# Closing a group of the GCN pass in steps between its turns, with the last layer's self edges taken from rows in SBUF

## The chip, the core and the metric

The kernel runs on one core of one Trainium2 chip. The metric is the device time of one execution in microseconds, lower is better. The engines are TensorE (PE), VectorE (DVE), ScalarE (ACT), GpSimd (POOL) and SyncE (SP); each works through its own instructions in order and waits for the others on semaphores.

## The reference, cut to what matters

A graph network over 12,500 nodes and 212,500 edges with 64 features: four layers, each of the form x = x + layer(relu(layernorm(x))). The change lies in the third layer and in what prepares the fourth:

```python
def _L2_gnn_ref(x, edge_index, W, b):          # third layer, GCN
    xw = x @ W
    norm = dis[src] * dis[dst]                 # src, dst with a loop for each node added
    out = segment_sum(norm[:, None] * xw[src], dst) + b
    return relu(out)

def _L3_gnn_ref(h, r, a, Wa_w, Wa_b, ...):     # fourth layer, four edge types
    cat = concatenate([h[dst], h[src]])
    gate = sigmoid(sum_i where(etype == i, cat @ r[i], 0))
    a_sc = sum(leaky_relu(cat @ Wa_w.T + Wa_b) * a[0])
    att = softmax of a_sc over the edges of a dst
    h_N = segment_sum(h[src] * att * gate, dst)
```

Among the fourth layer's edges are self edges (src equal to dst). The kernel does not gather those: it computes them for a whole block of nodes and opens the layer's running sums (`rel_state`, with the running maximum `rel_top`) with them.

## The kernel before

Nodes stand in 98 blocks of 128, one node a partition, sorted by degree. A block's edges are cut into chunks of four slots for 128 nodes; a chunk is fetched by four gathers (indirect DMAs that POOL issues, L973), each of one row per partition. Four chunks make a turn (RING = 4), and `got` holds the four chunks of a turn. SP loads a turn's lists of row numbers in two stages of two chunks (`load_lists`, L952) and its block numbers (`meta`, L957). DVE takes the chunks in order: it waits until one has landed, gives its list back (`list_used`), adds its four slots (L1709), gives the buffer back (`got_free`) and adds the sum to the block's state (L1712). SP's next list load waits for `list_used`, POOL for the list and for `got_free`.

The GCN pass (`gcn_edges`) does this first for the short chunks of two slots, then for the long ones. In the long part the turns are cut into 7 groups by blocks: when the turns of group g are done, the sums of 14 blocks are whole, and they are closed at once, as tiles of 128 x 896 (14 blocks of 64):

- `close(g)` on DVE: scale by `dis`, add the bias, relu and add to x (L1726 to L1729), then `relu_norm` (L405 to L414, with a square root on ACT in between), a copy to h (L1734), and the signal `h_ready`.
- PE transposes `hg` (L1793); for each of the 14 blocks it makes the source part `p_s` and the own part `p_w` of the last layer's rows (L1801 to L1803).
- ACT copies each block from PSUM into `rows` and `own` in SBUF (L1833 to L1839, the last raises `taken`) and sends them out as tables (L1841, L1843). There are seven such buffers.
- PE then makes the products of the self edges, `p_f`, with w_loop = w_src + w_own, two blocks in flight (L1808, L1810).
- `own_edges(g)` on DVE: for each block it takes p_f and makes the score and the gate (L1746 to L1755, with the four types' logits times `loop_type` and added up); then for all 14 the tanh on ACT (L1821) and the writes of `last_top` and `last_state` (L1759 to L1770).

DVE's order is written out: the turns of group g, then own_edges(g - 1), then close(g), then the turns of group g + 1. After the last group come own_edges(5), close(6) and own_edges(6), with no gathers beside them, and then the last layer (`rel_edges`), whose first gather needs the tables.

Of the kernel before, what the change touches and what calls it, by code (L numbers as in the profile page):

```python
# [7 lines left out]
ALU = mybir.AluOpType  # L8
# [113 lines left out]
def one_block(nc, eng):  # L122

    eng.addr_align(LOOP_SLOTS, max_nops=16)
# [15 lines left out]
def bc(ap, shape):  # L140
    return ap.to_broadcast(shape)
# [259 lines left out]
def relu_norm(nc, dve, ch, x, h, sq, st, shape, var_ready, std_ready, n):  # L401


    wide = lambda j: bc(st[:, j, :].unsqueeze(2), shape)
    ch.link(nc.vector.tensor_reduce(st[:, 0, :], x, AX, ALU.add))  # L405
    ch.link(nc.vector.tensor_scalar(st[:, 3, :], st[:, 0, :], 1.0 / D, None, ALU.mult))
    ch.link(nc.vector.tensor_tensor(h, x, wide(3), ALU.subtract))
# [3 lines left out]
    dve.wait_ge(std_ready, n)  # L411
    ch.link(nc.vector.reciprocal(st[:, 3, :], st[:, 2, :]))
    ch.link(nc.vector.tensor_scalar(sq, h, 0.0, None, ALU.max))
    ch.link(nc.vector.tensor_tensor(h, sq, wide(3), ALU.mult))  # L414
# [737 lines left out]
def load_weights(nc, k, a):  # L1152


    with ExitStack() as ctx:
# [55 lines left out]
        def _(dve):  # L1211
# [37 lines left out]
            ch.link(nc.vector.tensor_tensor(k.w_loop[:, :], k.w_src[:, :], k.w_own[:, :], ALU.add))  # L1249
# [103 lines left out]
def group_turns(eng, lists, g):  # L1353

    return (eng.value_load(lists.row_i[0:1, 9, bass.ds(g, 1)], min_val=0, max_val=CHUNKS // RING - 2),
            eng.value_load(lists.row_i[0:1, 9, bass.ds(g + 1, 1)], min_val=1, max_val=CHUNKS // RING - 2))
# [295 lines left out]
def gcn_edges(nc, k, part, state, table, after):  # L1652
# [4 lines left out]
    HELD = GROUP // 2  # L1657
    with ExitStack() as ctx:
# [3 lines left out]
        if after:  # L1662
            x, h, dis, bias, last_state, last_top = after
            logit, score = m.sb("logit", [P, TYPES, D]), m.sb("score", [P, D])
            gate, tanh = m.sb("gate", [P, GROUP, D]), m.sb("tanh", [P, GROUP, D])
            own_e, half_loop = m.sb("own_e", [P, GROUP]), m.sb("half_loop", [P, GROUP])
            p_f = [m.ps(f"p_f{j}", [P, OROW]) for j in range(2)]
            loop_made, loop_used = m.sem("loop_made"), m.sem("loop_used")
            gate_ready, tanh_ready = m.sem("gate_ready"), m.sem("tanh_ready")
            full = [P, GROUP, D]  # L1670
            Y, sq, hg = m.sb("Y", full), m.sb("sq", full), m.sb("hg", full)
            st = m.sb("st", [P, 4, GROUP])
# [4 lines left out]
            rows = [m.sb(f"rows{j}", [P, TYPES, RROW]) for j in range(HELD)]  # L1677
            own = [m.sb(f"own{j}", [P, OROW]) for j in range(HELD)]
# [3 lines left out]
            out = [m.sem(f"out{j}") for j in range(HELD)]  # L1682
# [14 lines left out]
        def _(dve):  # L1697
# [22 lines left out]
            def close(g):  # L1720
# [12 lines left out]
                relu_norm(nc, dve, ch, xb, hg[:, :, :], sq[:, :, :], st, full, var_ready, std_ready, g + 1)  # L1733
                ch.link(nc.vector.tensor_copy(h[:, blocks, :], hg[:, :, :]))  # L1734
                dve.sem_inc(h_ready, 1)

            def own_edges(g):
# [4 lines left out]
                for j in range(GROUP):  # L1742
                    z = j % 2
                    dve.wait_ge(loop_made, g * GROUP + j + 1)
                    dve.sem_inc(r.tick, 1)
                    ch.add(nc.vector.scalar_tensor_tensor(out=score[:, :], in0=p_f[z][:, 0:D], scalar=0.0,  # L1746
                                                          in1=k.att_a99[:, :], op0=ALU.max, op1=ALU.mult))
                    ch.link(nc.vector.tensor_tensor(logit[:, :, :], p_f[z][:, AW:].rearrange("p (t d) -> p t d", t=TYPES),
                                                    bc(k.loop_type[:, bass.ds(g * GROUP + j, 1), :]
                                                       .rearrange("p b t -> p (b t)").unsqueeze(2), [P, TYPES, D]),  # L1750
                                                    ALU.mult))
                    ch.add(nc.vector.tensor_reduce(own_e[:, j:j + 1], score[:, :], AX, ALU.add))
                    ch.link(nc.vector.tensor_reduce(gate[:, j, :], logit[:, :, :].rearrange("p t d -> p d t"), AX,
                                                    ALU.add))
                    ch.link(nc.vector.tensor_tensor(own_e[:, j:j + 1], own_e[:, j:j + 1], p_f[z][:, D:AW], ALU.add))  # L1755
                    dve.sem_inc(loop_used, 1)
                dve.sem_inc(gate_ready, 1)
# [15 lines left out]
            def group(g):  # L1773
                t0, t1 = group_turns(dve, lists, g)
                one_block(nc, dve)
                with dve.Fori(t0, t1) as i:
                    turn(i)

            group(0)
            close(0)  # L1780
            with dve.Fori(1, TURNS) as g:
                group(g)
                own_edges(g - 1)
                close(g)
            own_edges(TURNS - 1)

        if after:
            @block.tensor
            def _(pe):
                with pe.Fori(0, TURNS) as g:  # L1790
# [14 lines left out]
                    for j in range(GROUP):  # L1805
                        y, z = j % 2, j % 2
                        pe.wait_ge(loop_used, g * GROUP + j + 1)
                        nc.tensor.matmul(p_f[z][:, :], hT[y * D:(y + 1) * D, j // 2, :], k.w_loop[y * D:(y + 1) * D, :],  # L1808
                                         start=True, stop=False)
                        nc.tensor.matmul(p_f[z][:, 0:AW], k.ones[y * D:y * D + 1, :], k.own_bias[y * D:y * D + 1, 0:AW],  # L1810
                                         start=False, stop=True).then_inc(loop_made, 1)

            @block.scalar
            def _(act):
                act.sem_inc(taken, 2)
                act.sem_inc(loop_used, 2)
                for j in range(HELD):
                    act.sem_inc(out[j], 32)
                def tanhs(g):
# [3 lines left out]
                def group(g):  # L1823
# [4 lines left out]
                    for j in range(GROUP):  # L1828
                        z, w = j % 2, j % HELD
# [3 lines left out]
                        nc.scalar.activation(rows[w][:, :, 0:AW], bc(p_s[z][:, 0:AW].unsqueeze(1), [P, TYPES, AW]),  # L1833
                                             ACT.Copy)
                        nc.scalar.activation(rows[w][:, :, AW:AW + D],
                                             p_s[z][:, AW:].rearrange("p (t d) -> p t d", t=TYPES), ACT.Copy)
                        nc.scalar.activation(rows[w][:, :, AW + D:RROW], bc(hg[:, j:j + 1, :], [P, TYPES, D]), ACT.Copy,
                                             scale=0.5)
                        nc.scalar.activation(own[w][:, :], p_w[z][:, :], ACT.Copy).then_inc(taken, 1)  # L1839
                        act.wait_ge(taken, g * GROUP + j + 3)  # L1840
                        act.dma_start(by_rank(k.rel_tab)[:, blk, :], rows[w][:, :, :].rearrange("p t c -> p (t c)")  # L1841
                                      .unsqueeze(1)).then_inc(out[w], 16)
                        act.dma_start(k.own_tab[blk].rearrange("a p c -> p (a c)"), own[w][:, :]).then_inc(out[w], 16)  # L1843
# [6 lines left out]
                for j in range(HELD):  # L1850
                    act.wait_ge(out[j], 64 * TURNS + 32)
# [457 lines left out]
def gnn_program(nc, a, out):  # L2309
    ctx = ExitStack()  # L2310
    with ctx:
# [34 lines left out]
        k.w_loop = m.sb("w_loop", [P, OROW])  # L2346
# [139 lines left out]
```

## Time and profile before

| | |
|---|---|
| median of 3 runs | 13329.96 us (13327.62 to 13337.75) |
| profiled execution | 13332.53 us, its span 13330.8 us |
| busy in the span | POOL 64%, DVE 47%, PE 17%, ACT 13%, PE weight loads 11% |
| GCN pass, gathers | 1640, from 8576.0 to 10813.4 us |
| last layer, first gather | 10947.8 us |

Busy shares are means over all layers, which have different limits; what a stop costs is read from the timeline of its own stretch. In the rows below an instruction stands with its start, its duration, its engine, its line, what it writes and reads, and in brackets how long the engine was idle before it and what ended that.

### The profile page before, as it was taken

To read this page: it belongs to the slowest core of one execution; us is meant where nothing else is said; L and a number is where in the kernel's file an instruction comes from. 1 tells how busy PE (TensorE), PEld (TensorE's weight loads), DVE (VectorE), ACT (ScalarE), POOL (GpSimd) and SP (SyncE) were. 2 spreads that over 40 slices of the span, in tenths; PEclk is the share of its full clock that TensorE was granted. 3 is DMA by queue.
4 is the path that set the end of the run, shared out by engine and by line. 5 is a ranking of instruction groups with operands and counts; after the bars stand their busy time and mean duration, and the time that the engine had idled before them with its cause. 6 is when DMAs were issued, how large, how long until landed. Compare 5 with 4: busy or idle time off the path is not lost. (4 is left out here: it accounts for less than half of the span.)

```text
span 13330.8 us, 107772 instructions
## 1 busy us (share of the span) xinstructions
PE 2243.3 (17%) x7664; PEld 1456.1 (11%) x7664; DVE 6297.5 (47%) x21149; ACT 1706.1 (13%) x5627; POOL 8506.9 (64%) x8805
## 2 busy tenths in 40 slices
PE   8730000000000000000000000012222233333334
PEld 6620000000000000000000000001111112222223
DVE  9992333333344444444444444312222237777765
ACT  0000000000001000000011111000000014444443
POOL 0017466677656767776767777676666647777775
PEclk9755555555555555555555555555555555555555
DMA  0001233333311222222111111122222224444442
GB/s 10 0 14 39 28 27 27 26 29 28 27 21 29 32 33 33 33 33 31 26 25 27 27 27 27 26 49 47 47 47 48 48 52 107 108 107 107 107 101 64
DMA packets 1006418, 574.69 MB, mean 43 GB/s; under 512 B 757826, under 2 KB 855635, under 8 KB 1005953
## 3 DMA queue, kind: packets, MB, share of 16 engines
q0 software_dynamic: 307520, 409.04, 18.8%
q1 hardware_dynamic: 587723, 101.69, 4.7%
q10 hardware_dynamic: 111088, 63.12, 1.6%
q14 instruction: 71, 0.58, 0.0%
q8 instruction: 16, 0.26, 0.0%
HBM read 485.71 MB, written 87.37 MB: 43 GB/s over the span
## 5 line engine op out<-in xcount | busy, mean ns | idle before, releaser
L973 POOL DMA_INDIRECT got<-gat_tab,list x3280 | 3113.8, 949 | 1323.4 <-issue 970.7
L973 POOL DMA_INDIRECT got<-rel_tab,list x1640 | 1648.0, 1005 | 709.3 <-issue 448.4
L973 POOL DMA_INDIRECT got<-gcn_tab,list x1640 | 1548.5, 944 | 740.6 <-issue 495.7
L973 POOL DMA_INDIRECT got<-h_tab,list x1640 | 1567.9, 956 | 676.1 <-issue 492.4
L1709 DVE TENSOR_REDUCE chunk_sum<-got 128x64 f32<-128x256 f32 (+1 forms) x436 | 239.7, 550 | 1577.2 <-DMA got<-gcn_tab,list 1492.7
L1059 DVE TENSOR_TENSOR prod<-got,h 128x256 f32<-128x256 f32 (+1 forms) x436 | 179.6, 412 | 1309.2 <-DMA got<-h_tab,list 1203.5
L1641 PE MATMUL p_t<-ident,hg 128*128 128x128 f32 x98 | 24.6, 429 | 4436.6 <-DVEq L1546 4436.6
L1446 DVE COPY e<-top 128x4 f32 (+1 forms) x872 | 189.3, 217 | 1224.1 <-DMA got<-gat_tab,list 966.6
L535 POOL DMA_INDIRECT info_tab<-info,rank_i x98 | 125.4, 1279 | 977.1 <-DVEq L512 947.5
L2204 PE MATMUL p_gate<-got,ident 128*128 128x256 f32 (+1 forms) x872 | 510.3, 689 | 1382.8 <-DVE gate L2041 1382.8
L1588 ACT ACTIVATE p<-e 128x20 f32<-128x20 f32 (+3 forms) x872 | 185.4, 213 | 3719.1 <-DVE e L1465 3536.9
L358 PE MATMUL counts<-hot 125*128 125x98 bf16 x3400 | 608.3, 356 | 70.6 <-DVE hot L256 70.6
L2041 DVE COPY_PREDICATED gate<-is_t,own 128x256 f32<-128x256 int32 (+1 forms) x1308 | 553.9, 423 | 45.2 <-issue 35.4
L1430 DVE SCALAR_TENSOR_TENSOR type_of<-list 128x4 f32<-128x4 int32 (+1 forms) x436 | 72.9, 167 | 965.8 <-DMA got<-gat_tab,list 908.1
L1641 PEld LDWEIGHTS p_t<-ident,hg 128*128 128x128 f32 x98 | 19.0, 223 | 4439.3 <-DVEq L1546 4439.3
L358 PEld LDWEIGHTS counts<-hot 125*128 125x128 bf16 x3400 | 478.1, 142 | 199.7 <-DVE hot L256 86.2
L1486 DVE TENSOR_REDUCE chunk_sum<-prod 128x68 f32<-128x272 f32 (+3 forms) x872 | 494.4, 567 | 1.1
L2174 ACT ACTIVATE value<-got,msg 128x64 f32<-128x64 f32 x1640 | 439.2, 336 | 14.1
L2206 PE MATMUL p_gate<-gate,ident 128*128 128x256 f32 (+1 forms) x872 | 440.3, 609 | 0.0
L1299 PE MATMUL p_t<-ident,staged 128*128 128x128 f32 x49 | 23.2, 473 | 2446.2 <-ACT staged L1315 2442.5
L2035 DVE TENSOR_TENSOR feat<-got,own 128x256 f32<-128x256 f32 (+1 forms) x436 | 179.0, 411 | 536.3 <-DMA got<-rel_tab,list 516.6
L2204 PEld LDWEIGHTS p_gate<-got,ident 128*128 128x128 f32 x872 | 218.2, 310 | 1674.6 <-DVE gate L2041 1674.6
(436 smaller groups left out, 8709.3 us busy)
## 6 DMA issues: line engine op xcount, KB each, us to landing
own<-own_tab SPq DMA_DIRECT2D x436, 160.5 KB, 2.4
got<-gat_tab,list POOLq DMA_INDIRECT x3280
rel_tab<-rows ACTq DMA_DIRECT2D x98, 386.0 KB, 2.9
got<-h_tab,list POOLq DMA_INDIRECT x1640
got<-gcn_tab,list POOLq DMA_INDIRECT x1640
got<-rel_tab,list POOLq DMA_INDIRECT x1640
own_tab<-own ACTq DMA_DIRECT2D x98, 160.5 KB, 3.4
chunks_src<-rows_src SPq DMA_DIRECT2D x480, 4.5 KB
```

What stands on the lines that cost most here:

```text
L358: last = nc.tensor.matmul(counts[j][:, :], hot[:, h, 0:P, t], hot[:, h, P:P + BLOCKS, t], start=False, stop=False, skip_group_check=True)
L973: pool.indirect_dma_start(r.got[:, q, j, :], None, table, at(r.lists[s][:, c, j:j + 1]))\
L1059: return ts.add(nc.vector.tensor_tensor(prod[:, :, :], r.got[:, q, :, 0:D], bc(own_hn[:, bass.ds(b[q], 1), :], [P, S, D]), ALU.mult))
L1446: ts.add(nc.vector.tensor_copy(e[:, z, S, :], top[:, blk, :].rearrange("p b h -> p (b h)")))
L1486: return ts.add(nc.vector.tensor_reduce(chunk_sum[:, :], prod[:, :, :].rearrange("p s f -> p f s"), AX, ALU.add))
L1588: nc.scalar.activation(p[:, q % 2, :, :], e[:, q % 2, :, :], ACT.Exp).then_inc(p_ready, 1)
L1709: ts.link(nc.vector.tensor_reduce(chunk_sum[:, :], r.got[:, q, :, :].rearrange("p s f -> p f s"), AX, ALU.add))
L2035: nc.vector.tensor_tensor(feat[:, q, :, :], r.got[:, q, :, 0:D], bc(own[:, q, 0:D].unsqueeze(1), [P, S, D]), ALU.add)\
L2041: ins = nc.vector.copy_predicated(gate[:, q, :, :], bc(is_t[:, t, q, :].unsqueeze(2), [P, S, D]), bc(own[:, q, AW + (t + 1) * D:AW + (t + ...
L2174: last = nc.scalar.activation(value[:, q, j, :], r.got[:, q, j, AW + D:RROW], ACT.Copy, scale=msg[:, q, j, D:AW])
L2204: nc.tensor.matmul(p_gate[z][:, :, :], k.ident[:, :], r.got[:, q, :, AW:AW + D], start=True, stop=False)
L2206: nc.tensor.matmul(p_gate[z][:, :, :], k.ident[:, :], gate[:, q, :, :], start=False, stop=True)\
```

## The change

`relu_norm` is split in two, `norm_variance` (up to the variance) and `norm_scale` (from the reciprocal on). A group's closing is no longer done at once, but in five steps between the turns of the next group: `sums` ahead of its first turn, `scale` after the first, `own_half` for seven blocks after the fourth, `own_half` for the other seven after the fifth, and `own_edges` after the sixth. Six turns of a group are therefore written out in the loop over groups, and the rest stays an inner loop. `h_ready` comes before the copy to h. `own_half` takes the score and gate of the self edges from `rows` and `own` in SBUF, which ACT fills anyway, for seven blocks (128 x 448) at a time, and picks the type with predicated copies. The products p_f, w_loop and their semaphores are gone; `rows` and `own` hold all 14 blocks.

```diff
-def relu_norm(nc, dve, ch, x, h, sq, st, shape, var_ready, std_ready, n):
+def norm_variance(nc, ch, x, h, sq, st, shape, var_ready):
...
+def norm_scale(nc, ch, h, sq, st, shape):
...
-            ch.link(nc.vector.tensor_tensor(k.w_loop[:, :], k.w_src[:, :], k.w_own[:, :], ALU.add))
...
-            rows = [m.sb(f"rows{j}", [P, TYPES, RROW]) for j in range(HELD)]
-            own = [m.sb(f"own{j}", [P, OROW]) for j in range(HELD)]
+            rows, own = m.sb("rows", [P, GROUP, TYPES, RROW]), m.sb("own", [P, GROUP, OROW])
...
-            def close(g):
+            def sums(g):
...
                 dve.wait_ge(taken, g * GROUP + 2)
                 dve.sem_inc(r.tick, 1)
-                relu_norm(nc, dve, ch, xb, hg[:, :, :], sq[:, :, :], st, full, var_ready, std_ready, g + 1)
-                ch.link(nc.vector.tensor_copy(h[:, blocks, :], hg[:, :, :]))
+                norm_variance(nc, ch, xb, hg[:, :, :], sq[:, :, :], st, full, var_ready)
+
+            def scale(g):
+                dve.sem_clear(close_step)
+                ch = Chain(dve, close_step)
+                dve.wait_ge(std_ready, g + 1)
+                dve.sem_inc(r.tick, 1)
+                norm_scale(nc, ch, hg[:, :, :], sq[:, :, :], st, full)
                 dve.sem_inc(h_ready, 1)
+                ch.link(nc.vector.tensor_copy(h[:, bass.ds(g * GROUP, GROUP), :], hg[:, :, :]))
+
+            def own_half(g, half):
+                js = slice(half * HALF, (half + 1) * HALF)
+                dve.sem_clear(close_step)
+                ch = Chain(dve, close_step)
+                dve.wait_ge(taken, g * GROUP + ((half + 1) * HALF + 2))
+                dve.sem_inc(r.tick, 1)
+                tt = nc.vector.tensor_tensor
+                ch.add(tt(score[:, :, :], rows[:, js, 0, 0:D], own[:, js, 0:D], ALU.add))
+                ch.add(nc.vector.tensor_copy(of_type[:, :, :],
+                                             k.loop_type[:, bass.ds(g * GROUP + half * HALF, HALF), :]))
+                ch.link(tt(gate[:, js, :], rows[:, js, 0, AW:AW + D], own[:, js, AW:AW + D], ALU.add))
+                ch.add(nc.vector.scalar_tensor_tensor(out=score[:, :, :], in0=score[:, :, :], scalar=0.0,
+                                                      in1=bc(k.att_a99[:, :].unsqueeze(1), [P, HALF, D]),
+                                                      op0=ALU.max, op1=ALU.mult))
+                for t in range(1, TYPES):
+                    ch.link(tt(logit[:, :, :], rows[:, js, t, AW:AW + D],
+                               own[:, js, AW + t * D:AW + (t + 1) * D], ALU.add))
+                    ch.link(nc.vector.copy_predicated(gate[:, js, :],
+                                                      bc(of_type[:, :, t].unsqueeze(2), [P, HALF, D]).bitcast(I32),
+                                                      logit[:, :, :]))
+                ch.link(nc.vector.tensor_reduce(own_e[:, js], score[:, :, :], AX, ALU.add))
+                ch.link(tt(own_e[:, js], own_e[:, js], rows[:, js, 0, D], ALU.add))
+                ch.link(tt(own_e[:, js], own_e[:, js], own[:, js, D], ALU.add))
...
-                for j in range(GROUP):
-                    z = j % 2
-                    dve.wait_ge(loop_made, g * GROUP + j + 1)
...
-            group(0)
-            close(0)
-            with dve.Fori(1, TURNS) as g:
-                group(g)
-                own_edges(g - 1)
-                close(g)
+            t0, t1 = group_turns(dve, lists, 0)
+            one_block(nc, dve)
+            with dve.Fori(t0, t1) as i:
+                turn(i)
+            with dve.Fori(1, TURNS) as g:
+                t0, t1 = group_turns(dve, lists, g)
+                sums(g - 1)
+                turn(t0)
+                scale(g - 1)
+                turn(t0 + 1)
+                turn(t0 + 2)
+                turn(t0 + 3)
+                own_half(g - 1, 0)
+                turn(t0 + 4)
+                own_half(g - 1, 1)
+                dve.sem_inc(gate_ready, 1)
+                turn(t0 + 5)
+                own_edges(g - 1)
+                one_block(nc, dve)
+                with dve.Fori(t0 + 6, t1) as i:
+                    turn(i)
+            sums(TURNS - 1)
+            scale(TURNS - 1)
+            own_half(TURNS - 1, 0)
+            own_half(TURNS - 1, 1)
+            dve.sem_inc(gate_ready, 1)
             own_edges(TURNS - 1)
...
-                    for j in range(GROUP):
-                        y, z = j % 2, j % 2
-                        pe.wait_ge(loop_used, g * GROUP + j + 1)
-                        nc.tensor.matmul(p_f[z][:, :], hT[y * D:(y + 1) * D, j // 2, :], k.w_loop[y * D:(y + 1) * D, :],
-                                         start=True, stop=False)
...
-                        act.wait_ge(out[w], g * 64 + (32 * (j // HELD) + 32))
+                        act.wait_ge(out[j], g * 32 + 32)
```

## Rows read from the trace of the kernel before

**Rows 1.** The page: busy time of the engines (us, share, instructions); the costliest groups
```profile
PE 2243.3 (17%) x7664; PEld 1456.1 (11%) x7664; DVE 6297.5 (47%) x21149; ACT 1706.1 (13%) x5627; POOL 8506.9 (64%) x8805
...
L973 POOL DMA_INDIRECT got<-gcn_tab,list x1640 | 1548.5, 944 | 740.6 <-issue 495.7
```

**Rows 2.** Waits of POOL, 8830 to 10947: total us, times, longest us
```profile
POOL got L973 <- DMA list<-chunks_rank: 177.9, 18, 34.5
```

**Rows 3.** Timeline, closing after group 1: start us, us, instruction [idle before, releaser]
```profile
9103.51 0.22 DVE L1712 TENSOR_TENSOR gcn_state<-gcn_state,chunk_sum 128x64 f32 x1 [0.24 <-DVE chunk_sum L1709]
...
9120.11 0.94 POOL L973 DMA_INDIRECT got<-gcn_tab,list  x1 [0.30 <-issue]
...
9151.61 0.58 DVE L1709 TENSOR_REDUCE chunk_sum<-got 128x64 f32<-128x256 f32 x1 [4.48 <-issue]
...
9153.01 2.83 SPq L952 DMA_DIRECT2D list<-chunks_rank  x2
...
9155.57 0.94 POOL L973 DMA_INDIRECT got<-gcn_tab,list  x1 [34.52 <-DMA list<-chunks_rank]
...
9158.58 0.94 POOL L973 DMA_INDIRECT got<-gcn_tab,list  x1 [2.07 <-issue]
```

**Rows 4.** Timeline, closing after group 0
```profile
8901.27 0.23 DVE L1712 TENSOR_TENSOR gcn_state<-gcn_state,chunk_sum 128x64 f32 x1 [0.24 <-DVE chunk_sum L1709]
...
8904.19 1.82 POOL L973 DMA_INDIRECT got<-gcn_tab,list  x1 [0.30 <-issue]
...
8907.57 1.04 POOL L973 DMA_INDIRECT got<-gcn_tab,list  x1 [0.30 <-issue]
...
8910.07 0.17 DVE L410 TENSOR_SCALAR st<-st 128x14 f32<-128x14 f32 x1
...
8912.72 0.63 DVE L1734 COPY h<-hg 128x896 f32<-128x896 f32 x1
...
8917.72 0.58 DVE L1709 TENSOR_REDUCE chunk_sum<-got 128x64 f32<-128x256 f32 x1 [4.38 <-issue]
...
8921.60 0.94 POOL L973 DMA_INDIRECT got<-gcn_tab,list  x1 [1.75 <-DMA list<-chunks_rank]
```

**Rows 5.** Timeline, gathers beside a closing of the second GAT layer
```profile
6881.04 1.76 POOL L973 DMA_INDIRECT got<-gat_tab,list  x1 [0.30 <-issue]
...
6889.34 1.17 POOL L973 DMA_INDIRECT got<-gat_tab,list  x1 [0.30 <-issue]
```

**Rows 6.** Groups by line and form, GCN pass and last layer: busy us, mean ns
```profile
L1748 DVE TENSOR_TENSOR logit<-p_f,loop_type 128x256 f32<-128x256 f32 x98 | 40.6, 415 | 0.0
...
L1753 DVE TENSOR_REDUCE gate<-logit 128x64 f32<-128x256 f32 x98 | 56.4, 576 | 0.0
...
L409 DVE TENSOR_REDUCE st<-sq 128x14 f32<-128x896 f32 x7 | 7.6, 1086 | 0.2
...
L2041 DVE COPY_PREDICATED gate<-is_t,own 128x256 f32<-128x256 int32 x1152 | 507.3, 440 | 38.7 <-issue 35.4
```

**Rows 7.** Timeline, end of the pass, DVE, PE, ACT and POOL
```profile
10815.82 0.23 DVE L1712 TENSOR_TENSOR gcn_state<-gcn_state,chunk_sum 128x64 f32 x1 [0.24 <-DVE chunk_sum L1709]
...
10847.76 1.09 DVE L1726 TENSOR_TENSOR Y<-gcn_state,dis 128x896 f32 x1 [0.29 <-DVE rel_state L1770]
...
10859.48 1.76 PE L1793 MATMUL p_t<-ident,hg 128*128 128x128 f32 x7 [17.50 <-DVEq L1735]
...
10905.94 0.44 ACT L1839 ACTIVATE own<-p_w 128x321 f32<-128x321 f32 x1
...
10934.25 0.15 DVE L1755 TENSOR_TENSOR own_e<-own_e,p_f 128x1 f32<-128x1 f32 x1
...
10937.02 1.09 DVE L1770 TENSOR_TENSOR rel_state<-gate,half_loop 128x896 f32<-128x896 f32 x1
...
10947.81 0.94 POOL L973 DMA_INDIRECT got<-rel_tab,list  x1 [134.40 <-DMA list<-chunks_rank]
```

**Rows 8.** DMA queues, 8830 to 10947: packets, MB, share of 16 engines
```profile
q14 instruction: 10, 0.08, 0.0%
```

More of the change, by code:

```diff
@@ L1663, in gcn_edges @@
             x, h, dis, bias, last_state, last_top = after
-            logit, score = m.sb("logit", [P, TYPES, D]), m.sb("score", [P, D])
-            gate, tanh = m.sb("gate", [P, GROUP, D]), m.sb("tanh", [P, GROUP, D])
+            logit, score = m.sb("logit", [P, HALF, D]), m.sb("score", [P, HALF, D])
+            of_type = m.sb("of_type", [P, HALF, TYPES])
             own_e, half_loop = m.sb("own_e", [P, GROUP]), m.sb("half_loop", [P, GROUP])
-            p_f = [m.ps(f"p_f{j}", [P, OROW]) for j in range(2)]
-            loop_made, loop_used = m.sem("loop_made"), m.sem("loop_used")
             gate_ready, tanh_ready = m.sem("gate_ready"), m.sem("tanh_ready")
@@ L1681, in gcn_edges @@
             made, taken = m.sem("made"), m.sem("taken")
-            out = [m.sem(f"out{j}") for j in range(HELD)]
+            out = [m.sem(f"out{j}") for j in range(GROUP)]
         block = ctx.enter_context(nc.Block())
@@ L1815, in _ @@
                 act.sem_inc(taken, 2)
-                act.sem_inc(loop_used, 2)
-                for j in range(HELD):
+                for j in range(GROUP):
                     act.sem_inc(out[j], 32)
@@ L1828, in group @@
                     for j in range(GROUP):
-                        z, w = j % 2, j % HELD
+                        z = j % 2
                         blk = bass.ds(g * GROUP + j, 1)
                         act.wait_ge(made, g * GROUP + j + 1)
-                        act.wait_ge(out[w], g * 64 + (32 * (j // HELD) + 32))
-                        nc.scalar.activation(rows[w][:, :, 0:AW], bc(p_s[z][:, 0:AW].unsqueeze(1), [P, TYPES, AW]),
+                        act.wait_ge(out[j], g * 32 + 32)
+                        nc.scalar.activation(rows[:, j, :, 0:AW], bc(p_s[z][:, 0:AW].unsqueeze(1), [P, TYPES, AW]),
                                              ACT.Copy)
-                        nc.scalar.activation(rows[w][:, :, AW:AW + D],
+                        nc.scalar.activation(rows[:, j, :, AW:AW + D],
                                              p_s[z][:, AW:].rearrange("p (t d) -> p t d", t=TYPES), ACT.Copy)
-                        nc.scalar.activation(rows[w][:, :, AW + D:RROW], bc(hg[:, j:j + 1, :], [P, TYPES, D]), ACT.Copy,
+                        nc.scalar.activation(rows[:, j, :, AW + D:RROW], bc(hg[:, j:j + 1, :], [P, TYPES, D]), ACT.Copy,
                                              scale=0.5)
-                        nc.scalar.activation(own[w][:, :], p_w[z][:, :], ACT.Copy).then_inc(taken, 1)
+                        nc.scalar.activation(own[:, j, :], p_w[z][:, :], ACT.Copy).then_inc(taken, 1)
                         act.wait_ge(taken, g * GROUP + j + 3)
-                        act.dma_start(by_rank(k.rel_tab)[:, blk, :], rows[w][:, :, :].rearrange("p t c -> p (t c)")
-                                      .unsqueeze(1)).then_inc(out[w], 16)
-                        act.dma_start(k.own_tab[blk].rearrange("a p c -> p (a c)"), own[w][:, :]).then_inc(out[w], 16)
+                        act.dma_start(by_rank(k.rel_tab)[:, blk, :], rows[:, j, :, :].rearrange("p t c -> p (t c)")
+                                      .unsqueeze(1)).then_inc(out[j], 16)
+                        act.dma_start(k.own_tab[blk].rearrange("a p c -> p (a c)"), own[:, j, :]).then_inc(out[j], 16)
                 group(0)
@@ L1849, in _ @@
                 tanhs(TURNS - 1)
-                for j in range(HELD):
-                    act.wait_ge(out[j], 64 * TURNS + 32)
+                for j in range(GROUP):
+                    act.wait_ge(out[j], 32 * TURNS + 32)
 def number_rows(nc, k, column):
```

33 lines of the change are left out of this document (9 added, 24 removed).

## The prediction

> **What bounds the kernel now.** I read the page first. POOL is the busiest engine, and its largest item in the GCN pass is the gather of L973: 1640 of them at 944 ns, with as many short idle stretches behind them [rows 1]. In the timeline one gather follows the other every 1.25 us (0.94 and 0.30 of issue [rows 3]), so a turn of 16 gathers takes 20 us and POOL paces the pass as long as it has lists and free buffers. The next view is the list of what POOL waited for: 18 waits for a list, 177.9 us together, the longest 34.5 [rows 2]. The third is the timeline around such a wait. After the last addition of group 1 (it ends at 9103.73, which I call T0) DVE runs own_edges(0) and close(1) and comes back to a chunk only at 9151.61; POOL, which had the lists of one turn in hand, issues its last gather at 9120.11 and the next at 9155.57 [rows 3]. The reader is to see the order at the end of that gap: DVE's first chunk sum, 1.40 us later SyncE's list load, 2.56 us later POOL. The list waits for DVE, because `list_used` comes from DVE. The last view is the end of the pass: from the last addition (10816.05) to the last write of the layer's state (10938.11) no gather runs, and POOL's idle there is 134.40 us [rows 7].
>
> So two things set the pass besides POOL's own 1.25 us a gather: the stops at the six closings inside it, and the chain behind the last gather.
>
> **The stops that go.** The 18 list waits hold 0.30 us each that every gather has, so 177.9 - 18 x 0.30 = 172.5 us are real stops; five of 34.5 and one of 1.75 [rows 2, 3, 4] make nearly all of it. One further gather behind the first stop waited 2.07 in place of 0.30 [rows 3]: 1.8. **Gain 174.3 us** if no stop is left. Whether one is left is a question of DVE's longest absence. When must it be back? POOL's next gather after T0 is due 1.25 after the one at 9120.11, at T0 + 17.63; from DVE's first chunk sum to that gather pass 3.96 us (9151.61 to 9155.57 [rows 3]). So the first chunk sum must start by T0 + 13.67.
>
> The steps of the change against that figure:
> - sums: in the closing after group 0 (T0 there is 8901.50) the same instructions end at 8910.24, 8.74 after T0. Going back to the turns took 4.37 (copy of h ends 8913.35, chunk sum 8917.72 [rows 4]); that holds the reading of the two turn numbers, which the new code does ahead of sums, and the start of a turn. Together 13.1: in time, with 0.6 to spare.
> - scale: 8910.24 to 8913.35 is 3.1, with 4.4 for the restart 7.5.
> - own_half: 448 elements a partition. A 256-element addition takes 415 ns and an 896-element one 1.09 us [rows 6, 7], so 448 take about 0.62; a predicated copy of 256 takes 440 [rows 6], so about 0.64 here; a reduction lies between 576 and 1086 [rows 6], 0.73. Six additions and products 3.7, three predicated copies 1.9, one reduction 0.7, three short ones 0.5, some 0.06 between instructions 0.8: 7.7 us, an estimate from those rows. Bounds: the 256-element durations all through give 5, the 896-element ones 12. With 0.3 and 4.4 around it: 12.4.
> - own_edges without its loop: 10934.40 to 10938.11 is 3.7 [rows 7]; with the restart 8.4.
>
> All stay under 13.67. Between steps DVE handles a chunk in 1.25 us of the 5 us that its four gathers take, so each turn begins with an empty backlog. If sums had no cover it would cost its own 13 us a closing. Queued behind the new `taken` waits are DVE's turns, hence lists and POOL; but hg is ready about T0 + 22.5 (one turn and scale), the row products and copies take 46.9 (10859.48 to 10906.38 [rows 7]), so they end at T0 + 70, while the second own_half is reached after five turns, at T0 + 100, and the first at T0 + 80 for half of them. These waits are past when DVE comes. The DMAs of ACT keep their number, size and queue; seven buffers more only take a wait away that does not appear. The removed products on PE (28 matmuls a group), the addition that made w_loop and the earlier h_ready lie beside POOL's gathers in the pass and count nothing there (the w_loop addition stands ahead of all layers and is worth some 0.5 us by the 256-element row, which I leave out).
>
> **What overlap costs.** In the old kernel most of a closing ran while POOL stood. Where DVE's 896-element work met gathers, some were longer: 1.82 and 1.04 in nine gathers [rows 4], 0.98 more than 0.94 each; 1.76 and 1.17 in a closing of the GAT layer [rows 5], 1.05 more. That is 0.11 a gather. The new closing keeps DVE at work for 8.5 + 3.1 + 15.4 + 3.7 = 30.7 us beside 24 gathers. For the half in 448-element instructions I take half the toll, since they hold for half the time: 12 x 0.11 + 12 x 0.055 = 2.0 us a closing, 12 in six, 11 beyond what closing 0 paid already. Bounds: 0 and 24 x 0.11 x 6 = 16, so 0 to 15 net.
>
> On this a page speaks against the change: the Trainium skill's "SBUF — State Buffer", section "Who interferes with whom", says that a VectorE instruction with two SBUF inputs and a GpSimd instruction that reads SBUF block each other for the whole instruction. The rows agree that something is lengthened, but two gathers of nine by 0.98 us is far from every instruction. The old own_edges read PSUM, the new own_half reads SBUF twice, so by that rule the new form is the worse one, and the sum would be that of rival 2, 13223; I go by the rows.
>
> **The end of the pass.** Old: 122.06 us from T0 to the last write [rows 7]. New: hg at T0 + 11.2 (8901.50 to 8912.72 [rows 4]), PE's start 0.1 later because h_ready now precedes the copy of h, 46.9 of row products and copies, 0.1, the second own_half 7.7 (the first runs under the copies), own_edges' rest 3.7: 69.7. **Gain 52.4 us**, bounds 48 to 55 by own_half. It comes from own_edges(5), which moved into the pass, and from the 28 us of loop products behind the last row copy (10906.38 to 10934.40 [rows 7]), which one own_half replaces.
>
> **The sum.** 174.3 + 52.4 - 11 = 215.7 us. The profiled execution took 13332.53 (span 13330.8), which becomes 13116.8; it lies 2.57 above the median of the runs shown, so the median should be near **13114 us**. With the bounds of overlap and own_half: 13100 to 13123.
>
> **Rivals.**
> 1. The 0.6 us of sums do not hold. A restart cost 4.37 and 4.48 us [rows 3, 4]; if the longer loop body costs a second one at the head of each pass, 4.4 - 0.6 = 3.8 us a closing, 23 in six: 13137. Against it: closing 0 was away for 16.2 us, 2.55 too long by the figure above, and the stop was 1.45 [rows 4]; two slow gathers, 0.98 together, had put the need off by that much, and would do so again. For it: six turns written out make the loop body much longer, and the old one loaded hardly any code, ten packets over the whole stretch [rows 8]. In the Trainium skill, "Runtime: NRT & Kernel Launch", section "Instruction fetch mechanics", a jump back beyond the two pages held must wait for a fetch; no run here shows the length of one.
> 2. The port decides: POOL is held for every two-input instruction. Per closing eight of 1.09 us and 2 x (6 x 0.62 + 3 x 0.64) = 11.3, 20 us; in six 120 in place of 11: 13223. Against it: rows 4 and 5 as above. This is the rule of the Trainium skill's "SBUF — State Buffer" taken at its word.
> 3. No change: the stop is only cut into pieces. Five steps in six closings would have to stop POOL for 215.7 / 30 = 7.2 us each, so every absence would be over 20.9 us. Closing 0, longer than any step, speaks against it; 13330.
> 4. Slower: DVE waits in own_half for `taken`, with the ring behind it. To pass 0.2% (27 us, about what a measurement of this kernel tells from no change) a closing must stop POOL for (215.7 + 27) / 6 = 40 us, so the copies would have to end 30 + 1 + 40 us later than T0 + 70: 14 blocks in 118 us, 8.4 a block. The rows say 46.9, 3.35 a block [rows 7], and nothing in the change touches that work's instructions. From 118 us on it would give 13357 and more.
>
> **How the numbers follow.** Forecast 0.76; rival 1 0.14; rival 2 0.04; rival 3 0.03; rival 4 0.02; 0.01 for faster than the bounds. The range 13098 to 13148 takes the forecast's bounds and rival 1 with some microseconds of run to run spread (the runs shown differ by 10). Faster by over 0.2%: 0.95, within 0.03, slower 0.02.
>
> **What will show it.** In the changed profile: POOL's list waits fall from 177.9 us to under 20; no gather in the pass idles over 5 us; DVE's first chunk sum after sums starts 12.5 to 13.7 after T0; own_half lasts 7 to 8.5 us; gathers' mean rises from 944 ns to about 950; POOL's idle before the last layer falls from 134 to about 82. I would be wrong if gathers beside own_half take well over 1 us each, if a stop of some microseconds stands at the head of each group, or if own_half begins with a wait.

## The result, and the profile after

The changed kernel takes 13128.97 us, the median of 4 runs (13124.81 to 13132.07), against 13328.79 us for the kernel before (median of 4 runs on the same chip): ratio 0.9849, with a 95% interval of 0.9832 to 0.9866. That is 200 us saved. It lies inside the predicted range (13098 to 13148) and 15 us above the forecast of 13114, also a little above the 13100 to 13123 given for the forecast alone.

The profiled execution is the one of 13127.03 us (span 13125.3, that is 205.5 less than before). The page, with the busy time of the engines and the group of the GCN gathers (busy us, mean ns, idle us before them), answers to [rows 1]:

```profile
PE 2049.2 (16%) x7272; PEld 1359.3 (10%) x7272; DVE 6252.4 (48%) x20840; ACT 1706.0 (13%) x5627; POOL 8520.1 (65%) x8805
...
L981 POOL DMA_INDIRECT got<-gcn_tab,list x1640 | 1561.6, 952 | 574.7 <-issue 493.6
```

The gathers of the pass now take 13.1 us longer in sum (1548.5 before, 1561.6 now) and POOL's idle time in front of them is 165.9 us shorter (740.6, now 574.7). POOL's waits inside the pass (total us, times, longest us) answer to [rows 2]:

```profile
POOL got L981 <- issue: 436.9, 1422, 2.1
POOL got L981 <- DMA list<-chunks_rank: 14.4, 26, 2.6
```

Twenty-six waits for a list are 14.4 us, where 18 were 177.9 (with the end of the pass left out in both). At 0.30 each, 6.6 us of that are stops. The timeline shows where they are. First the closing after group 0, beside [rows 4], then that after group 1, beside [rows 3]:

```profile
8905.04 0.22 DVE L1717 TENSOR_TENSOR gcn_state<-gcn_state,chunk_sum 128x64 f32 x1 [0.24 <-DVE chunk_sum L1714]
...
8907.33 1.09 DVE L1732 TENSOR_TENSOR Y<-gcn_state,dis 128x896 f32 x1 [2.07 <-issue]
...
8917.76 0.58 DVE L1714 TENSOR_REDUCE chunk_sum<-got 128x64 f32<-128x256 f32 x1 [1.89 <-issue]
...
9107.46 0.22 DVE L1717 TENSOR_TENSOR gcn_state<-gcn_state,chunk_sum 128x64 f32 x1 [0.24 <-DVE chunk_sum L1714]
...
9112.97 1.09 DVE L1732 TENSOR_TENSOR Y<-gcn_state,dis 128x896 f32 x1 [5.29 <-issue]
...
9123.46 0.58 DVE L1714 TENSOR_REDUCE chunk_sum<-got 128x64 f32<-128x256 f32 x1 [1.89 <-issue]
...
9127.57 0.94 POOL L981 DMA_INDIRECT got<-gcn_tab,list  x1 [2.61 <-DMA list<-chunks_rank]
...
9130.58 0.94 POOL L981 DMA_INDIRECT got<-gcn_tab,list  x1 [2.07 <-issue]
```

The reader is to measure from the end of the last addition, T0, to the first chunk sum. In the first closing that is 8905.26 to 8917.76, 12.5 us, and POOL doesn't stop. In the second it is 9107.68 to 9123.46, 15.8 us, and POOL stops for 2.61. The difference is in one place: DVE's idle time before the first instruction of `sums`, 2.07 us in the first pass of the loop over groups and 5.29 in the second, put down to "issue", so to nothing that DVE waited for. The list of DVE's waits shows that the other passes are like the second: six times with 27.7 us together, so 5.1 on average in the last five, and DVE is away for 15.4 to 15.8 us in each of them. The other four stops are shorter, 1.33 to 1.38 us: there one gather beside `sums` was itself lengthened by 0.8 to 0.9 us (one of them is shown further down), so POOL needed its list that much later; in the second closing none was. The same list has the waits of `own_half` for the row copies:

```profile
DVE score L1760 <- ACT own L1870: 39.5, 2, 25.1
DVE Y L1732 <- issue: 27.7, 6, 5.3
```

Only two of these exist, and the next view shows that both belong to the last closing. It is the timeline of the end of the pass, beside [rows 7]:

```profile
10666.86 0.23 DVE L1717 TENSOR_TENSOR gcn_state<-gcn_state,chunk_sum 128x64 f32 x1 [0.24 <-DVE chunk_sum L1714]
...
10678.46 1.75 PE L1831 MATMUL p_t<-ident,hg 128*128 128x128 f32 x7 [345.35 <-DVEq L1748]
...
10704.18 0.62 DVE L1760 TENSOR_TENSOR score<-rows,own 128x448 f32<-128x448 f32 x1 [25.05 <-ACT own L1870]
...
10725.50 0.63 DVE L1760 TENSOR_TENSOR score<-rows,own 128x448 f32<-128x448 f32 x1 [14.43 <-ACT own L1870]
...
10732.23 0.17 DVE L1775 TENSOR_TENSOR own_e<-own_e,own 128x7 f32<-128x7 f32 x1
...
10734.92 1.09 DVE L1794 TENSOR_TENSOR rel_state<-Y,half_loop 128x896 f32<-128x896 f32 x1
...
10746.00 0.94 POOL L981 DMA_INDIRECT got<-rel_tab,list  x1 [81.51 <-DMA list<-chunks_rank]
```

From the last addition (10667.09) to the last write (10736.01) it is 68.9 us in place of 122.06, and POOL's idle time before the last layer is 81.5 in place of 134.4. With that the whole difference is accounted for: 165.9 of idle time in the pass, less 13.1 of longer gathers, plus 52.9 at its end is 205.7 of the 205.5 us of the span.

Last the instruction loads, 9200 to 10600 (packets, MB, share of 16 engines). In the kernel before, the queue has no packet from 9200 to 10900, and [rows 8] has 10 for the whole stretch; now there are:

```profile
q14 instruction: 22, 0.18, 0.0%
```

Two of them move in the idle time ahead of `sums` in each of the last five passes, in the first pass none. For the second pass, from 9107.7 to 9113 us:

```profile
q14 instruction: 2, 0.02, 0.9%
```

### The profile page after: what moved, and what is told of

Read it like the earlier page. It is cut to its first block and busy times, and to the rows that moved or that the text cites. A ratio compares the mean times of both kernels' runs of the same rounds, so it can differ in the third digit from the quotient of the medians.

```text
span 13125.3 us, 106291 instructions
## 1 busy us (share of the span) xinstructions
PE 2049.2 (16%) x7272; PEld 1359.3 (10%) x7272; DVE 6252.4 (48%) x20840; ACT 1706.0 (13%) x5627; POOL 8520.1 (65%) x8805
## 5 line engine op out<-in xcount | busy, mean ns | idle before, releaser
L981 POOL DMA_INDIRECT got<-gcn_tab,list x1640 | 1561.6, 952 | 574.7 <-issue 493.6
L1481 DVE TENSOR_TENSOR prod<-got,p 128x272 f32<-128x272 f32 (+3 forms) x872 | 366.1, 420 | 60.8 <-ACT p L1595 59.9
```

The lines of the kernel that those rows point to most:

```text
L981: pool.indirect_dma_start(r.got[:, q, j, :], None, table, at(r.lists[s][:, c, j:j + 1]))\
L1481: weighed = ts.add(nc.vector.tensor_tensor(prod[:, :, :].rearrange(hc, h=heads), r.got[:, q, :, 0:HW].rearrange(hc, h=heads), bc(p[:, z, 0 ...
```

## The experiments

My theory: the 15 us missing are the stops left by the late start of `sums`, and this start is late because the longer loop body has to be loaded anew at each jump back. The rival: the start of a group costs that much whatever the body's length, or the missing time is the gathers' own, held by DVE's instructions. A second question was how much each half of the change (the steps, the self edges from SBUF) is worth alone. The first four kernels and the last two ran beside the kernel before, each group on one chip (13327.12 us median of 7 runs, and 13331.85 of 9). The three in between have one run each, beside a single run of the kernel before of 13306.91 us, so only rows inside them are compared.

**e1_at_once.** The self edges come from SBUF, but the closing is done at once, in the old order.

```diff
+            def group(g):
+                t0, t1 = group_turns(dve, lists, g)
+                one_block(nc, dve)
+                with dve.Fori(t0, t1) as i:
+                    turn(i)
...
             with dve.Fori(1, TURNS) as g:
...
+                group(g)
                 own_half(g - 1, 0)
...
                 own_half(g - 1, 1)
                 dve.sem_inc(gate_ready, 1)
...
                 own_edges(g - 1)
...
+                sums(g)
+                scale(g)
```

> One part alone: self edges from the rows in SBUF, but a closing done at once behind its group's turns, in the old order. If both parts carry the gain (my account): DVE is away for 2 x 6.9 + 3.7 + 11.6 + 4.4 = 33.5 us, 19.8 over the 13.67 it may be, at five closings, and the end of the pass gets one own_edges and two halves more, 18 us: list waits in the long part near 115 us, POOL's idle ahead of the last layer near 100, time near 13128 + 92 + 18 = 13238. If the form of the self edges is what gained and the steps between turns do nothing, it stays at 13130.

Measured: 13235.51 us (13230.15 to 13237.95), ratio 0.993 [0.9914, 0.9947]. The timeline at the closing after group 1:

```profile
9106.18 0.22 DVE L1717 TENSOR_TENSOR gcn_state<-gcn_state,chunk_sum 128x64 f32 x1 [0.24 <-DVE chunk_sum L1714]
...
9141.53 0.58 DVE L1714 TENSOR_REDUCE chunk_sum<-got 128x64 f32<-128x256 f32 x1 [4.38 <-issue]
...
9145.66 0.94 POOL L981 DMA_INDIRECT got<-gcn_tab,list  x1 [21.18 <-DMA list<-chunks_rank]
```

DVE is away for 35.1 us in place of the 47.9 of [rows 3], and POOL stops for 21.18 in place of 34.52: the stop shrinks by what the absence does (13.3 and 12.8). Up to the first gather of the last layer POOL's waits for a list are

```profile
POOL got L981 <- DMA list<-chunks_rank: 211.5, 21, 99.7
```

The form from SBUF alone, with every closing still stopping POOL, is worth 92 us of the 200.

**e2_pf_steps.** The steps between turns, but the self edges are still PE's products, seven blocks to a step.

```diff
             def own_half(g, half):
...
+                for j in range(half * HALF, (half + 1) * HALF):
+                    z = j % 2
+                    dve.wait_ge(loop_made, g * GROUP + j + 1)
+                    dve.sem_inc(r.tick, 1)
+                    ch.add(nc.vector.scalar_tensor_tensor(out=score[:, :], in0=p_f[z][:, 0:D], scalar=0.0,
+                                                          in1=k.att_a99[:, :], op0=ALU.max, op1=ALU.mult))
...
+                    dve.sem_inc(loop_used, 1)
```

> The other part alone: the closing in steps between turns, but the self edges from products on PE, seven blocks a step. My account: a half is 7 x 1.98 = 13.9 us, with 4.7 around it 18.6, so each half stops POOL for about 5 us, 60 in twelve, and the end of the pass is longer by 28 - 7 = 21: time near 13205. If the steps alone carry the gain, whatever a half costs, the pass keeps its 13130 and only the end is longer: 13150.

Measured: 13162.79 us (13159.22 to 13166.76), ratio 0.9878 [0.9861, 0.9894]; lower than the 13205 that I expected. The timeline of one of its steps:

```profile
8987.83 0.22 DVE L1763 SCALAR_TENSOR_TENSOR score<-p_f,att_a 128x64 f32<-128x64 f32 x1 [0.32 <-DVE gcn_state L1719]
...
9001.10 0.15 DVE L1772 TENSOR_TENSOR own_e<-own_e,p_f 128x1 f32<-128x1 f32 x1
...
9003.43 0.58 DVE L1716 TENSOR_REDUCE chunk_sum<-got 128x64 f32<-128x256 f32 x1 [2.17 <-issue]
...
9007.40 0.94 POOL L981 DMA_INDIRECT got<-gcn_tab,list  x1 [2.60 <-DMA list<-chunks_rank]
```

A step of seven blocks lasts 13.4 us, but the return to the turns costs 2.2 us and not the 4.4 that I took from [rows 3, 4]. The 4.4 held the reading of turn numbers and the start of a loop, which a step in written-out code doesn't have. So the step is 15.9 us away, not 18, and the stop is 2.60. POOL's waits for a list up to the last layer are here

```profile
POOL got L981 <- DMA list<-chunks_rank: 134.6, 33, 102.3
```

102.3 us of that are the end of the pass; the other 32 come to 32.3, so at 0.30 each 22.7 us of stops. The steps alone are worth 164 us of the 200. The halves add up to 256: they shorten the same stops, so each is worth less behind the other.

**e3_sums_later.** `sums` goes behind the group's first turn, and `scale` behind the second.

```diff
                 t0, t1 = group_turns(dve, lists, g)
-                sums(g - 1)
                 turn(t0)
-                scale(g - 1)
+                sums(g - 1)
                 turn(t0 + 1)
+                scale(g - 1)
```

> One turn ahead of sums, all else as in the change. If the stops left at groups 1 to 5 come from the jump back to the head of the loop over groups (DVE stands 5.1 to 5.3 us ahead of sums there, 2.1 at the first pass), the jump falls into a turn, where DVE has 4 us to spare a chunk: the idle ahead of sums falls under 1 us, DVE is away about 10.5 us, no list wait over 0.5 us is left, and the pass is 8 us shorter than in the change (first to last gather 2085 to about 2077). If sums and the start of a turn are too long wherever they stand, stops of 1 us or more stay.

Measured: 13111.33 us (13106.21 to 13113.67), ratio 0.9837 [0.9821, 0.9854]. The page's group of gathers; POOL's waits to the end of the pass; DVE's waits before `sums`; the head of a group in the timeline:

```profile
L981 POOL DMA_INDIRECT got<-gcn_tab,list x1640 | 1557.4, 950 | 564.7 <-issue 492.5
```
```profile
POOL got L981 <- DMA list<-chunks_rank: 87.9, 22, 81.5
```
```profile
DVE Y L1732 <- DVE gcn_state L1717: 2.6, 7, 0.5
```
```profile
9104.64 0.23 DVE L1717 TENSOR_TENSOR gcn_state<-gcn_state,chunk_sum 128x64 f32 x1 [0.24 <-DVE chunk_sum L1714]
...
9111.58 0.58 DVE L1714 TENSOR_REDUCE chunk_sum<-got 128x64 f32<-128x256 f32 x1 [6.72 <-issue]
```

Between 9200 and 10600 the same 22 packets are still loaded, and the idle time at the head of a group is still there (6.72 us ahead of the turn), but it no longer adds to `sums`, which now starts after 0.37 us on average. The 22 list waits are 81.5 for the end of the pass and 0.30 for each other: no stop is left. POOL's idle time falls by 10.0 us (574.7 to 564.7). That is just what the changed kernel had left: five stops, 6.6 us above 0.30 each, and two gaps of 2.07 behind a stop, 3.5. So the cost at the head of a group does harm only where `sums` stands right behind it. The gathers are shorter too, by 4.2 us (1561.6 to 1557.4), so the pass gains 14.2 us and not the 8 that I expected. The intervals of the two ratios overlap; that e3 beats the change rests on these rows, and on e8 below, which ran beside the change.

**e4_short_body.** The order of the change, but turns two to four are an inner loop: fewer instructions in the body, with the same work.

```diff
-                turn(t0 + 1)
-                turn(t0 + 2)
-                turn(t0 + 3)
+                with dve.Fori(t0 + 1, t0 + 4) as i:
+                    turn(i)
                 own_half(g - 1, 0)
```

> The second to fourth turn of a group in an inner loop of three, so that the loop over groups holds five written turns, not seven. If DVE's instructions are loaded anew in each pass because the body is too long to stay, fewer or no instruction packets come in the later groups (22 between 9200 and 10600 us in the change), the idle ahead of sums falls towards 2 us at every group, and the stops go, some 8 us in all. If the wait ahead of sums is owed to the jump back whatever the body's length, it stays at 5.1 us and the stops with it.

Measured: 13117.39 us (13113.80 to 13124.36), ratio 0.9843 [0.9827, 0.986]. DVE's waits before `sums`, and the page's group of gathers:

```profile
DVE Y L1732 <- issue: 14.0, 6, 2.4
```
```profile
L981 POOL DMA_INDIRECT got<-gcn_tab,list x1640 | 1565.6, 955 | 564.6 <-issue 491.6
```

No instruction packet is left between 9200 and 10600, the idle time before `sums` is 2.07 us in the first pass and 2.4 in the other five, DVE is away for 12.5 to 12.8 us, and POOL's idle time is that of e3. The rival that a group's start costs 5 us whatever the body falls. The gathers are 8.2 us longer here than in e3: in the timeline 18 of them take over 1.3 us, in e3 eight, because the closing's instructions now fall otherwise on the gathers' beat: six gathers begin under the first instruction of `sums` and six under the last product of `scale` and are lengthened by 8.0 us together, where e3 has 0.2. What lengthens a gather is asked by the next three.

**e5_two_inputs, e6_one_input, e7_copies.** e3 with extra instructions of 896 elements a partition ahead of turn t0 + 3, whose results nothing uses: eight products of two SBUF inputs, eight reductions of one input, or fourteen copies. Their time on DVE is nearly the same (8.98, 8.93 and 9.23 us a closing).

```diff
+            def padding():
+                dve.sem_clear(close_step)
+                ch = Chain(dve, close_step)
+                for _ in range(8):
+                    ch.link(nc.vector.tensor_tensor(Y[:, :, :], hg[:, :, :], hg[:, :, :], ALU.mult))
...
                 turn(t0 + 2)
+                padding()
                 turn(t0 + 3)
```

> e3 with eight more instructions in each of the six closings, behind the third written turn: products of hg with itself, two SBUF inputs, 128 x 896, 1.09 us each, results not used. DVE is away for 9 + 2 us there, so no list wait. If a gather that starts while DVE works on two SBUF inputs is held until that instruction ends, as the starts and ends of the long gathers in the changed kernel suggest, POOL's busy time in the pass rises from 1557 by about 1 us a closing, 5 to 10 in all, in single gathers of 1.5 us and more. If gathers are longer merely because DVE is busy, it rises as in e6.

> e3 with eight more instructions at the same place of the same length, but with one input: reductions of hg, 128 x 896 to 128 x 14, results not used. If the second SBUF input is what holds a gather, POOL's busy time stays within 1 us of e3's 1557. If DVE's being busy is enough, it rises by 5 us or more as in e5.

> e3 with fourteen copies of hg at the same place, 128 x 896 in 0.63 us each (the fast form), results not used. Beside the single fast instructions of the closings gathers kept 0.94 to 0.96 us, which says that POOL's busy time stays near 1557. If such an instruction keeps POOL out for as long as it runs, it rises by 3 us a closing or more, and DVE's copies take longer than 0.63.

Measured: one run each, of 13110.45, 13094.76 and 13094.66 us. The gathers of the pass by the three pages of the profile:

```profile
L981 POOL DMA_INDIRECT got<-gcn_tab,list x1640 | 1574.4, 960 | 564.0 <-issue 492.8
```
```profile
L981 POOL DMA_INDIRECT got<-gcn_tab,list x1640 | 1560.6, 952 | 564.2 <-issue 493.8
```
```profile
L981 POOL DMA_INDIRECT got<-gcn_tab,list x1640 | 1560.4, 951 | 564.3 <-issue 494.9
```

The timeline of each beside the extra instructions of the first closing:

```profile
8942.65 8.98 DVE L1782 TENSOR_TENSOR Y<-hg 128x896 f32<-128x896 f32 x8
...
8942.84 1.71 POOL L981 DMA_INDIRECT got<-gcn_tab,list  x1 [0.30 <-issue]
...
8944.86 0.95 POOL L981 DMA_INDIRECT got<-gcn_tab,list  x1 [0.31 <-issue]
...
8946.11 1.83 POOL L981 DMA_INDIRECT got<-gcn_tab,list  x1 [0.30 <-issue]
```
```profile
8944.14 8.93 DVE L1782 TENSOR_REDUCE st<-hg 128x14 f32<-128x896 f32 x8
8944.45 0.95 POOL L981 DMA_INDIRECT got<-gcn_tab,list  x1 [0.31 <-issue]
8945.70 0.94 POOL L981 DMA_INDIRECT got<-gcn_tab,list  x1 [0.30 <-issue]
```
```profile
8944.66 9.23 DVE L1782 COPY Y<-hg 128x896 f32<-128x896 f32 x14
8944.99 1.11 POOL L981 DMA_INDIRECT got<-gcn_tab,list  x1 [0.30 <-issue]
8946.41 1.01 POOL L981 DMA_INDIRECT got<-gcn_tab,list  x1 [0.30 <-issue]
```

The first product ends 8942.65 + 1.09 = 8943.74, and the gather that began in it ends at 8944.55, 0.81 later. The gather at 8944.86 begins as the second product ends and the third has not begun, and takes its 0.95. The one at 8946.11 begins in the fourth and takes 1.83. Beside the reductions every gather takes 0.94 or 0.95. Beside the copies (0.66 us apart, so the first one ends near 8945.29) the first gather ends 0.81 after it, at 8946.10, and the others take 1.01 or 1.02. The reading that fits all three: a gather that begins while DVE runs an instruction with two SBUF inputs, or such a copy, is held until that instruction ends and takes some 0.82 us from there; a short instruction therefore costs it little (0.07 here), a long one up to 0.9, and a reduction nothing. Over all six closings 34 gathers begin under one of the products: 18 are held, and 16 begin in a product's last 0.01 us and are not. All 42 that begin under a copy are lengthened, by 3.6 us together; of the 45 that begin under a reduction none takes over 0.95. Products in place of reductions cost POOL 1574.4 - 1560.6 = 13.8 us, 2.3 a closing.

My expectations missed in size. e5 is 17.0 us above e3's 1557.4, not 5 to 10, and 14.8 of it stand beside the products. e6 is 3.2 above e3, not within 1: that comes from `own_half`, whose gate additions of 448 elements now meet the beginning of more gathers (4.4 us in place of 1.5), not from the reductions. e7 is 3.0 above, between the two values that I gave. DVE is hardly slowed by the extra instructions (8.98 us for the products, 8.93 for the reductions); the closing's one instruction that is lengthened by more than a tenth is the fast one-input product of `scale` (0.63 us with no gather beside it, up to 0.87 in the changed kernel).

This is the rule that the Trainium skill's "SBUF — State Buffer", section "Who interferes with whom", states (a second SBUF input, or a copy in its two-port mode, shares a port with GpSimd, one input doesn't), and these rows agree with it: nearly all of the cost falls on POOL here.

**after_again and e8_last_piece**, five runs each on one chip. The first is the changed kernel, unaltered. The second is e3 with the last group's second half of `own_half` divided into five blocks and two, so that only two blocks are left to do when ACT's last copy is made; `own_part(g, lo, n)` is `own_half` for n blocks from block lo.

```diff
...
-            own_half(TURNS - 1, 0)
-            own_half(TURNS - 1, 1)
+            own_part(TURNS - 1, 0, HALF)
+            own_part(TURNS - 1, HALF, 5)
+            own_part(TURNS - 1, HALF + 5, 2)
```

> The change once more, unaltered, to stand beside e8 on one chip: 13129, some 200 under the kernel before.

> e3 (one turn ahead of sums), and behind the last group the second half of the self edges in two pieces, five blocks and then two. If the last piece alone lies behind the last row copy, the end of the pass loses the difference between 6.9 us for seven blocks and about 3.6 for two: POOL's idle ahead of the last layer 81.5 to about 78, time near 13108, some 20 under the change. If the pieces cost as much as they hide, 81.5 stays and e3's 13111.

Measured: the changed kernel 13123.45 us (13119.49 to 13125.86), ratio 0.9844 [0.9831, 0.9857]; e8 13109.65 us (13101.86 to 13112.69), ratio 0.9832 [0.9819, 0.9846]. POOL's waits for a list in the one and in the other:

```profile
POOL got L981 <- DMA list<-chunks_rank: 92.5, 18, 81.3
```
```profile
POOL got L981 <- DMA list<-chunks_rank: 83.0, 16, 78.4
```

The longest, the wait at the end of the pass, falls by 2.9 us, and the others come down to 4.6 us for 15, so 0.31 each: no stop. The runs of the two don't overlap; e8 is 13.8 us faster than the change and beats both kernels, though the intervals of the two ratios still touch. How much of that is the last piece and how much the later `sums` is told by the waits alone (2.9 us against the 9.4 by which POOL's idle time in the pass falls, 573.1 to 563.7 by the pages of the profile); e3 and e8 ran on different chips.

## Why the prediction was right, and where it was short

**What bounds the kernel: right.** Taking DVE's absence away took POOL's stops away, and where the absence was only shortened (e1) the stop shrank with it (13.3 us for 12.8). The requirement that the first chunk sum starts by T0 + 13.67 holds: 12.5 and, in e4, 12.8 gave no stop, 15.8 gave 2.61.

**The stops that go: 165.9 us of the 174.3.** The step that failed is "in time, with 0.6 to spare" for `sums`. In the first pass the restart came out as foreseen, only in two places (2.07 us ahead of `sums` and 1.89 behind it, 12.5 after T0 in all where I had 13.1). In the other five the part ahead is 5.1, 3.1 more, where 1.2 us were to spare (13.67 less 12.5). I had that as rival 1, with 3.8 us a closing and 23 us in all. Its mechanism is shown (two instruction packets in each of the five idle times; e4: a shorter body, no packets, 2.4 us, no stop), its size is smaller: 10.1 us of stops and gaps in five closings, and the first pass has none. Two of the signs that I gave thus came out against me: the first chunk sum starts 15.4 to 15.8 us after T0 in five closings, not by 13.7, and a stop stands at the head of each of these groups. The sum had missed 1.8 of such gaps in the kernel before as well, since there were two of 2.07 and I counted one: 10.1 - 1.8 = 8.3, the shortfall but for rounding. This agrees with the Trainium skill's "Runtime: NRT & Kernel Launch", section "Instruction fetch mechanics": a jump back to code that is no longer held waits for its fetch. Here that is 3.1 us a jump more than in the first pass.

**The other steps: shorter than taken.** `own_half` lasts 6.9 us (10725.50 to 10732.40) where I had 7.7 (and 7 to 8.5 as a sign), and the return from a step in written-out code is 1.9 to 2.2 and not 4.4. Neither matters here, as these steps had room. `taken` is never waited for inside the pass, as worked out.

**What overlap costs: 13.1 us against 11 net, rightly sized by the wrong spread.** I had halved the toll for 448-element instructions because they hold for half the time, 4.0 us in six closings, and put 8 on the rest. The gathers beside `own_half` take 0.94 to 1.10 in all six closings, 2.4 us more together; beside 896-element instructions with two inputs they take up to 1.8, and some 11 us of the toll are there. A line from the first closing, and two from the third:

```profile
9011.89 1.05 POOL L981 DMA_INDIRECT got<-gcn_tab,list  x1 [0.30 <-issue]
...
9358.99 1.09 DVE L1734 TENSOR_TENSOR Y<-Y,v_L_gnn_b 128x896 f32<-128x896 f32 x1
9359.08 1.82 POOL L981 DMA_INDIRECT got<-gcn_tab,list  x1 [0.30 <-issue]
```

The DVE instruction ends at 9360.08 and the gather at 9360.90, 0.82 later, the same as in e5. Counted in the timeline, 12 gathers of the pass take over 1.3 us and are 9.4 us longer together than at 0.945; some 50 between 0.96 and 1.3 add 4.5. The sum came out near by luck: the toll is a matter of when a gather begins, as the experiments show, and not the 0.11 a gather that I had taken from two closings. Rival 2 (POOL held for the whole of each two-input instruction, 120 us) falls: a gather that began before the instruction is not held, and most instructions meet no beginning.

**The end of the pass: 52.9 us against 52.4.** hg came 11.3 us after T0 (11.2 foreseen), and the second `own_half` began 47.0 us after PE (46.9 of row products and copies). e1 shows 99.7 for the closing's end with own_edges(5) still there, and e2 102.3 with it gone but PE's products kept: each edit is worth some 32 to 35, both 52.9.

**Rivals 3 and 4.** No change needed steps that each stop POOL for 7 us; the longest stop is 2.61. The slower case needed a wait for `taken` inside the pass, and there is none.

**The 15 us.** Stops and gaps 8.4, the gathers 2.1 more than taken, the end of the pass 0.5 to the good: 10.0 of the 10.2 by which the profiled execution is above the 13116.8 of the sum. The other 4.5 are between executions: I had put the old profile 2.57 above its median, and the new one is 1.94 below its own. The step moved out of the way (e3) brought 13327.12 - 13111.33 = 215.8 us, where the sum had 215.7; that is close by some luck, since e3's gathers took 8.9 us more than before and not 11.

## What to carry to other kernels

Work out how long the engine that hands back lists or buffers may be away before its consumer stops (here 13.7 us), cut the long job into steps under that, and leave more spare than a jump back to code that has to be loaded costs (3.1 us here). The step that stands at the head of a loop body carries the loop's own cost too, so the shortest step, or plain work that has a backlog, belongs there, and a body grown by writing turns out is to be checked for instruction packets in its queue. Where a sum of two parts is credited to a change, time each alone: here they were worth 92 and 164 us, and 200 together.

## What the runs showed of the hardware that was not expected

- The jump back in a loop whose body had grown from one loop of turns to six written out costs DVE 5.1 us ahead of the first instruction, against 2.07 to 2.4 with nothing to load; 22 instruction packets from 9200 to 10600 go with it, two of them in each such idle time (none in the shorter body of e4). The longer body of e2 shows 5.0 us. How the length sets this was not measured beyond these bodies.
- A gather that begins under a two-input DVE instruction ends 0.82 us after that instruction, whatever was left of it (8943.74 to 8944.55, 9360.08 to 9360.90), and keeps its 0.94 where 0.12 us or less was left; one that began before it is not lengthened. Behind the last product of `scale` it is 0.97 us in the changed kernel; the cause of that stays open. Its cost thus depends on the beat of both: 8 gathers of over 1.3 us in e3, 18 in e4, with the same instructions in another order, 8.2 us apart in the pass.
